# Attention rows fetched by indirect DMA and DMA transposes instead of one-hot matmuls, in blocks 1 to 7

## The chip, the cores and the metric

The kernel runs on one core of a Trainium2 chip. The metric is the device time of one execution in microseconds (us); the time of a kernel is the median of its runs. All times in the trace are microseconds from the start of the execution's span.

## The reference

The model is one layer over 16 sequences of 256 tokens with a vocabulary of 128 and a width of 512:

```python
h = rms_norm(rms_norm(emb[x]) * norm_w @ proj_w.T)          # depends on the token id only
h = h + attention(layernorm(h))                             # 16 heads of 32
h = h + ffn(layernorm(h))                                   # hidden 2048
# attention: q, k = feature_map(heads of h @ W.T);  scores = (q . k) ** 2, causal
# o = scores @ v / (sum(scores) + eps);  o @ Wo.T
# ffn: x = fwht(x * SU_ug) / 64;  silu(x @ Wg.T * s) * (x @ Wu.T * s);  fwht; x @ Wd.T
```

There are no positions in q and k, so the squared score of two tokens depends on their ids alone. A 128 x 128 table per head, id against id, holds every score that can occur. For a block of 512 tokens the attention of a head needs, for each query token, the row of the table that belongs to its id, weighted by how often each key id has occurred up to that token in its sequence.

## The kernel before

Tokens are worked on in 8 blocks of 512 (two sequences each). After a set-up stage that loads and turns the weights and builds the tables, an attention stage for block 0 runs alone (phase 0 below). Then in each step the feed-forward of block b runs beside the attention of block b + 1: step 0 also turns the rest of the weights (phase 1 below), steps 1 to 6 are a loop, and the last step has block 7's feed-forward alone. Each step is cut into 32 slots, and in every slot each engine's program holds the pieces of both tasks in a fixed, hand-written order; semaphores join the engines. Slots 0 to 15 hold the gate and up products of one 128-wide tile of the hidden layer (24 matmuls of 128x512 on TensorE, `feed_half`), slots 16 to 31 a quarter of an output tile of the down product (12 matmuls).

The attention table `att` holds each head's scores as two f16 halves, high and low, whose sum is the score. In the kernel before, TensorE picks the rows: `att[:, half, h, :]` against the one-hot matrix `onehotT` of the block's ids (L1215 and L1216, two matmuls of 128x512 a head, 16 heads a block). They add the halves in PSUM (`PICK`). Then for each head, one a slot:

- DVE multiplies the picked rows by the counts `cnt` into `prod` (L674), f32;
- ACT copies `prod` to the f16 high half in `p16` (L855), POOL subtracts for the low half (L358);
- at slots 4, 8, 12 and 15 TensorE multiplies a quad of four heads by the values (L1231, 48 small matmuls); DVE divides by the sums, ACT and POOL split the result into halves, and SP turns it with a DMA transpose (L276) for the output projection in slots 18 to 24.

Beside it the feed-forward of a slot runs TensorE (gate, up), ACT's silu (L993), DVE's product `a` (L743), ACT's high half and POOL's low half (L398). DVE's `a` of a slot waits for POOL's low half of the slot before, and TensorE's slot s + 2 waits for `a` of slot s.

In slots 17 to 29 the rest of attention (residual, layer norm, a Walsh-Hadamard turn) goes row tile by row tile: POOL gathers the residual rows by an indirect DMA (L387), DVE normalises, SP turns the tile by a DMA transpose (L283), TensorE mixes it. SP's queue is in order: four turns of the attention output, then turns of tiles between the stores of the output (L303).

Phase 1 is crowded on DVE: besides the product and `a` it splits turned weights (L477, L499) and mixes the down weights in place (L491, L492).

## Time and profile before

| | us |
|---|---|
| median of 3 runs | 1402.48 |
| lowest and highest | 1400.31, 1403.24 |
| the profiled execution's own time | 1400.2 |
| its span | 1398.4 |
| TensorE busy in the span | 1306.7 (93%) |
| VectorE (DVE), ScalarE (ACT), GpSimd (POOL) busy | 532.3, 398.7, 422.9 |
| one step of the loop (block 2 on), from the windows | 149.4 |

The busy share of TensorE is not spread evenly: the trace has set-up and phase 0 until about 163 us, phase 1 until about 372, six steps of about 149.5, and the last feed-forward. A matmul's own duration is longer than the distance at which matmuls follow one another, since they are pipelined; what a matmul costs a full TensorE is that distance. The mean granted TensorE clock is 0.974 of full speed.

### The profile page before, as it was taken

What the parts mean: (1) busy time and instruction counts of PE and PEld (TensorE: products, weight loads), DVE (VectorE), ACT (ScalarE), POOL (GpSimd) and SP (SyncE); (2) the same over time, 40 slices, a digit from 0 to 9 for tenths busy, and PEclk for the clock granted to TensorE, in tenths of its full rate; (3) what the DMA queues carried; (4) which work ended last, traced back from release to release, by engine and by line L of the source; (5) the groups of instructions that cost most, each with busy time, mean ns of one, the idle gap of its engine ahead of it and who ended that gap; (6) DMA issues with size and microseconds to landing.
All of it is one profiled execution on the core that took longest, in us unless ns stands there. A gap on an engine that the chain in (4) does not pass through costs nothing.

```text
span 1398.4 us, 19203 instructions
## 1 busy us (share of the span) xinstructions
PE 1306.7 (93%) x7481; PEld 643.6 (46%) x7481; DVE 532.3 (38%) x1049; ACT 398.7 (29%) x703; POOL 422.9 (30%) x371
## 2 busy tenths in 40 slices
PE   5575598989999999999999999999999999999999
PEld 3352255554444444444444444444444444444444
DVE  1655567654422253226222432234222523251110
ACT  4453463440233113321233023311322123211220
POOL 0342143332144313432244213421433124321210
PEclk9888699999999999999999999999999999999999
DMA  8911100002100130003000210012001300020000
GB/s 297 288 27 23 24 1 9 8 8 54 53 8 9 31 75 8 15 15 80 19 16 8 68 38 8 15 42 64 8 8 23 83 8 15 15 68 23 0 0 30
DMA packets 101681, 55.73 MB, mean 40 GB/s; under 512 B 74180, under 2 KB 90872, under 8 KB 101112
## 3 DMA queue, kind: packets, MB, share of 16 engines
q1 hardware_dynamic: 98112, 45.77, 12.8%
q0 software_dynamic: 2560, 8.39, 2.0%
q8 instruction: 43, 0.70, 0.2%
q10 hardware_dynamic: 952, 0.75, 0.2%
q14 instruction: 14, 0.11, 0.0%
HBM read 29.47 MB, written 8.65 MB: 27 GB/s over the span
## 4 chain that ended last, share of the span: by engine, by line
PE 83%; DVE 6%; DMA 4%; ACT 4%; issue 2%; POOL 1%; SPq 0%; DVEq 0%; ACTq 0%
PE bank L1078 24%; PE bank L1079 24%; PE bank L1080 23%; DMA prod<-sg 3%; PE bank L1231 3%; PE bank L1073 2%; PE bank L1216 2%; PE bank L1215 2%; PE bank L1121 1%; DMA hid<-in_L_tok_norm_weight 1%; PE bank L1240 1%; ACT xT L855 1%; DVE wgu L477 1%; PE bank L1071 1%; ACT wgu L855 1%
## 5 line engine op out<-in xcount | busy, mean ns | idle before, releaser
L1078 PE MATMUL bank<-xT,wgu 128*128 128x512 f16 x1024 | 389.3, 380 | 1.4 <-DVE xT L708 1.4
L1079 PE MATMUL bank<-xT,wgu 128*128 128x512 f16 x1024 | 389.3, 380 | 0.0
L1080 PE MATMUL bank<-xT,wgu 128*128 128x512 f16 x1024 | 389.2, 380 | 0.0
L398 POOL TENSOR_TENSOR hid<-a,hid 128x512 f16<-128x512 f32 x128 | 147.9, 1156 | 512.0 <-ACT hid L855 512.0
L743 DVE SCALAR_TENSOR_TENSOR a<-bank,kap,sg 128x512 f32<-128x512 f32 x128 | 96.0, 750 | 477.5 <-PE bank L1080 324.4
L1078 PE MATMUL bank<-wd,hid 128*128 128x512 f16 x512 | 194.3, 379 | 0.0
L1079 PE MATMUL bank<-wd,hid 128*128 128x512 f16 x512 | 194.1, 379 | 0.0
L1080 PE MATMUL bank<-wd,hid 128*128 128x512 f16 x512 | 194.0, 379 | 0.0
L358 POOL TENSOR_TENSOR p<-prod,p 128x512 f16<-128x512 f32 x128 | 153.2, 1199 | 128.4 <-ACT p L855 128.4
L855 ACT ACTIVATE hid<-a 128x512 f16<-128x512 f32 x128 | 80.6, 630 | 279.5 <-DVE a L743 279.5
L1080 PEld LDWEIGHTS bank<-xT,wgu 128*128 128x128 f16 x1024 | 100.4, 98 | 121.6 <-issue 1.4
L1078 PEld LDWEIGHTS bank<-xT,wgu 128*128 128x128 f16 x1024 | 100.6, 98 | 119.9 <-DVE xT L708 2.3
L1079 PEld LDWEIGHTS bank<-xT,wgu 128*128 128x128 f16 x1024 | 100.4, 98 | 116.9 <-issue 1.1
L993 ACT ACTIVATE sg<-bank,sc 128x512 f32<-128x512 f32 x128 | 87.2, 681 | 134.0 <-PE bank L1080 77.9
L855 ACT ACTIVATE p<-prod 128x512 f16<-128x512 f32 x128 | 79.6, 626 | 133.0 <-PE bank L1231 111.9
L855 ACT ACTIVATE sg<-wide,rstd 128x512 f16<-128x512 f32 x32 | 23.1, 722 | 273.8 <-DVE wide L449 226.5
L674 DVE TENSOR_TENSOR prod<-bank,cnt 128x512 f32<-128x512 f32 x128 | 86.6, 681 | 8.7 <-ACT cnt L855 8.0
L332 POOL TENSOR_TENSOR rstd<-ve,mhalf 128x1 f32<-128x1 f32 x32 | 32.3, 1009 | 155.9 <-DVE ve L726 155.9
L1080 PEld LDWEIGHTS bank<-wd,hid 128*128 128x128 f16 x512 | 50.2, 98 | 60.5 <-issue 0.3
L1079 PEld LDWEIGHTS bank<-wd,hid 128*128 128x128 f16 x512 | 50.1, 98 | 60.3 <-issue 0.7
L1078 PEld LDWEIGHTS bank<-wd,hid 128*128 128x128 f16 x512 | 50.1, 98 | 60.2 <-issue 0.7
L717 DVE SCALAR_TENSOR_TENSOR h<-bank,gl,h_row 128x512 f32 (+1 forms) x28 | 21.0, 749 | 106.6 <-DMA h_row<-h_table,ids_c 106.6
(178 smaller groups left out, 1245.8 us busy)
## 6 DMA issues: line engine op xcount, KB each, us to landing
out<-a SPq DMA_DIRECT2D x24, 256.0 KB, 2.2
wgu<-in_L_ffn_W_gate SPq DMA_DIRECT2D x16, 256.0 KB, 5.5
wgu<-in_L_ffn_W_up SPq DMA_DIRECT2D x16, 256.0 KB, 5.0
wd<-in_L_ffn_W_down SPq DMA_DIRECT2D x4, 1024.0 KB, 9.4
ids_b<-in_x SPq DMA_DIRECT2D x8, 256.0 KB, 3.5
out<-h_row SPq DMA_DIRECT2D x8, 256.0 KB, 2.0
xT<-in_L_tok_proj_weight SPq DMA_DIRECT2D x1, 1024.0 KB, 8.6
p<-in_L_attn_Wq SPq DMA_DIRECT2D x1, 1024.0 KB, 13.8
```

The source lines that it names most:

```text
L332: return nc.gpsimd.tensor_tensor(dst, src, mhalf[:, 0:src.shape[1]], ALU.pow)
L358: nc.gpsimd.tensor_tensor(p16[:, 1, h % 4, :], prod[:, h % 2, :], p16[:, 0, h % 4, :], ALU.subtract)\
L398: nc.gpsimd.tensor_tensor(hid[:, 1, s, :], a32[:, :], hid[:, 0, s, :], ALU.subtract)\
L674: nc.vector.tensor_tensor(prod[:, s % 2, :], PICK[s % 2][:, :], cnt[:, :], ALU.mult)\
L743: nc.vector.scalar_tensor_tensor(a32[:, :], bank[:, :], kap[:, s:s + 1], sg[:, :], ALU.mult, ALU.mult).then_inc(S["a_done"], 1)
L855: return nc.scalar.activation(dst, src, ACT.Copy, **kw)
L993: nc.scalar.activation(sg[:, :], bank[:, :], ACT.Silu, scale=sc[:, s:s + 1]).then_inc(S["silu_done"], 1)
L1073: last = mm(bank[:, i * P:(i + 1) * P], pieces(i), rights(i), start=True, stop=True)
L1078: mm(dst, w[0], v[0], start=first, stop=False)
L1079: mm(dst, w[0], v[1], start=False, stop=False)
L1080: return mm(dst, w[1], v[0], start=False, stop=final)
L1231: last = mm(HEADS[m // 2][:, 4 * (m % 2) + j, :], p16[:, p, j, m * P:(m + 1) * P], val[:, w, 4 * q + j, :], start=first, stop=final, skip_ ...
```

## The change

The four tables of a quad of heads (128 ids x 1024 f16 values: two halves of four heads) are stored once in DRAM (`att_tables`). For blocks 1 to 7, and each quad q and each tile m of 128 tokens, POOL gathers 128 rows of 2 KB by an indirect DMA into a staging buffer, and SP turns them by a DMA transpose into `PB[q % 2]`, which is the memory of `att` for even quads and `p16` for odd ones. That is 16 gathers and 16 turns a block. Quad 0 of the next block goes through the buffer `ids_b` at slots 12, 14, 18 and 25 (`NEXT_AT`); quads 1 to 3 use four pieces of `hid` that the feed-forward fills from slot 12 on, at slots 0 and 1, 3 and 4, 7 and 8 (`FETCH_AT`).

TensorE's picks of blocks 1 to 7 are left out (block 0 keeps them). DVE adds the two halves into `prod` and then multiplies by `cnt`: two operations in place of one, all operands in SBUF. DVE's one-hot of the ids by rows, and its load, stay for block 0 alone. POOL's loop over the steps 1 to 6 is written out, so that the numbers it waits for are constants.

```diff
@@ tables, stages @@
+        onehot = onehotT[:, :].rearrange("p (c v) -> p c v", c=4)
+        p_even = att[:, :, :, :].rearrange("p l h v -> p (l h v)").rearrange("p (l j t) -> p l j t", l=2, j=4)
+        PB = [p_even, p16]
+        stages = [ids_b[:, :].bitcast(F16)]
+        stages += [hid[:, l, f:f + 2, :].rearrange("p a b -> p (a b)") for f in (FT - 2, FT - 4) for l in range(2)]
+FETCH_AT = {0: ((1, 0), (1, 1)), 1: ((1, 2), (1, 3)), 3: ((2, 0), (2, 1)), 4: ((2, 2), (2, 3)),
+            7: ((3, 0), (3, 1)), 8: ((3, 2), (3, 3))}
+NEXT_AT = (12, 14, 18, 25)
@@ SP @@
+            def p_turn(n, q, m):
+                way, g = fetched(n, q, m)
+                sp.wait_ge(S[f"pg_land{way}"], 16 * g + 16)
+                if n == 1 and q == 0 and m == 0:
+                    sp.wait_ge(S["tab_stored"], 64)
+                    sp.wait_ge(S["picked"], H)
+                if m == 0 and (n, q) != (1, 0):
+                    sp.wait_ge(S["heads_ready"], QUADS * n + q - 1)
+                nc.sync.dma_start_transpose(PB[q % 2][:, :, :, m * P:(m + 1) * P].rearrange("p l j t -> p (l j) t"),
+                                            stages[way]).then_inc(S[f"pt_land{way}"], 16)
...
-            load_ids_rows(1)
+            load_gather_ids(1)
+            store_tables()
             for q in range(QUADS):
+                if q == 3:
+                    for m in range(2):
+                        p_turn(1, 0, m)
                 o_turn(0, q)
+            p_turn(1, 0, 2)
             for m in range(4):
+                if m == 3:
+                    p_turn(1, 0, 3)
                 x_turn(0, m)
@@ POOL @@
+            def gather(n, q, m):
+                way, g = fetched(n, q, m)
...
+                if q == 1 and m == 0 and not first(n - 1):
+                    pool.wait_ge(S["y_ready"], 4 * n - 4)
+                if not (first(n - 1) and (q == 1 or q == 0 and m == 0)):
+                    pool.wait_ge(S[f"pt_land{way}"], 16 * g)
+                nc.gpsimd.indirect_dma_start(stages[way], None, att_tables[q],
+                                             bass.IndirectOffsetOnAxis(ids_p[:, m:m + 1].bitcast(U32), axis=0))\
+                    .then_inc(S[f"pg_land{way}"], 16)
@@ DVE, product(n, s), blocks 1 to 7 @@
-                    nc.vector.tensor_tensor(prod[:, s % 2, :], PICK[s % 2][:, :], cnt[:, :], ALU.mult)\
+                        raw = PB[s // 4 % 2]
+                        if s % 4 == 0:
+                            for m in range(4) if s else (3,):
+                                way, g = fetched(n, s // 4, m)
+                                dve.wait_ge(S[f"pt_land{way}"], 16 * g + 16)
...
+                        nc.vector.tensor_tensor(prod[:, s % 2, :], raw[:, 0, s % 4, :], raw[:, 1, s % 4, :], ALU.add)\
+                            .then_inc(S["ps_done"], 1)
...
+                        nc.vector.tensor_tensor(prod[:, s % 2, :], prod[:, s % 2, :], cnt[:, :], ALU.mult)\
@@ TensorE, attend(n, s) @@
-                for h in (0, 1) if s == 0 else (s + 1,) if s + 1 < H else ():
+                for h in () if not zero else (0, 1) if s == 0 else (s + 1,) if s + 1 < H else ():
```

How the change moves instructions, at three places. TensorE in the loop, at the end of slot 0's up product, before:

```order
L1080 MATMUL bank<-xT,wgu 128x512
L1203 MATMUL bank<-c,p 128x256
L1204 MATMUL bank<-c,p 128x128
L1203 MATMUL bank<-c,p 128x256
L1204 MATMUL bank<-c,p 128x128
...
L1215 MATMUL bank<-onehotT,att 128x512
L1216 MATMUL bank<-onehotT,att 128x512
L1215 MATMUL bank<-onehotT,att 128x512
L1216 MATMUL bank<-onehotT,att 128x512
L1078 MATMUL bank<-xT,wgu 128x512
```

The same place after:

```order
L1305 MATMUL bank<-c,onehotT 128x256
L1306 MATMUL bank<-c,onehotT 128x128
L1305 MATMUL bank<-c,onehotT 128x256
L1306 MATMUL bank<-c,onehotT 128x128
L1178 MATMUL bank<-xT,wgu 128x512
```

The count matmuls stay, the four picks are gone; slots 1 to 14 of every block from 1 on lose two picks each in the same way.

DVE in phase 1, between the end of slot 5 and the start of slot 6 (`wd` is the down weights, `wgu` the gate and up weights, `a` the feed-forward's product), before:

```order
L491 TENSOR_TENSOR wd<-wd 128x2x512
L492 SCALAR_TENSOR_TENSOR wd<-wd 128x2x512
L674 TENSOR_TENSOR prod<-bank,cnt 128x512
L477 TENSOR_TENSOR wgu<-bank,wgu 128x512
L743 SCALAR_TENSOR_TENSOR a<-bank,kap,sg 128x512
```

and after:

```order
L567 TENSOR_TENSOR wd<-wd 128x2x512
L568 SCALAR_TENSOR_TENSOR wd<-wd 128x2x512
L765 TENSOR_TENSOR prod<-p 128x512
L770 TENSOR_TENSOR prod<-prod,cnt 128x512
L553 TENSOR_TENSOR wgu<-bank,wgu 128x512
L839 SCALAR_TENSOR_TENSOR a<-bank,kap,sg 128x512
```

The add L765 is a new row ahead of the multiplication, in front of the weight's low half and of `a`; the same happens in every slot from 0 to 15.

SP's queue for phase 0 (the turns of `h_row` and of `sg` are block 0's own attention output and tiles), before:

```order
L265 DMA ids_b<-in_x 128x512
L276 DMA_TRANSPOSE oT<-h_row 128x8x128 x4
L283 DMA_TRANSPOSE prod<-sg 128x8x128 x4
L270 DMA ids_c<-in_x 128x4x1
L276 DMA_TRANSPOSE oT<-h_row 128x8x128 x4
```

and after:

```order
L282 DMA att_table<-att 256x1x512 x4
L309 DMA_TRANSPOSE oT<-h_row 128x8x128 x3
L297 DMA_TRANSPOSE att<-ids_b 128x8x128 x2
L309 DMA_TRANSPOSE oT<-h_row 128x8x128
L297 DMA_TRANSPOSE att<-ids_b 128x8x128
L316 DMA_TRANSPOSE prod<-sg 128x8x128 x3
L297 DMA_TRANSPOSE att<-ids_b 128x8x128
L316 DMA_TRANSPOSE prod<-sg 128x8x128
L303 DMA ids_c<-in_x 128x4x1
L297 DMA_TRANSPOSE p<-hid 128x8x128 x4
```

Two of block 1's first four turns now stand ahead of the last turn of block 0's output, one ahead of the first tile's turn and one ahead of the last tile's.

## Rows read from the trace of the kernel before

**Rows 1.** The page: busy time by engine, and the chain that ended last.

```profile
PE 1306.7 (93%) x7481; PEld 643.6 (46%) x7481; DVE 532.3 (38%) x1049; ACT 398.7 (29%) x703; POOL 422.9 (30%) x371
...
PE 83%; DVE 6%; DMA 4%; ACT 4%; issue 2%; POOL 1%; SPq 0%; DVEq 0%; ACTq 0%
```

**Rows 2.** Windows, two loop steps: engines' busy us, clock, DMA share, GB/s.

```profile
522.50:671.90 149.40, 148.77 (x862) 69.93 (x860) 51.72 (x106) 37.73 (x61) 49.28 (x44) 1.00 0.13 30
671.90:821.30 149.40, 148.77 (x861) 69.81 (x860) 51.72 (x106) 37.73 (x61) 49.32 (x44) 1.00 0.12 31
```

**Rows 3.** Timeline of TensorE in a loop step: start, duration, instruction.

```profile
563.43 0.38 PE L1215 MATMUL bank<-onehotT,att 128*128 128x512 f16 x1
563.65 0.38 PE L1216 MATMUL bank<-onehotT,att 128*128 128x512 f16 x1
563.86 0.38 PE L1078 MATMUL bank<-xT,wgu 128*128 128x512 f16 x1
```

**Rows 4.** The gathers L387: min/median/max ns, and landing.

```profile
L387 POOL DMA_INDIRECT h_row<-h_table,ids_c x28: 998/1054/1063, 329.1 to 1247.9; - x28
...
DMA to landing us min/median/max: 3.2/3.4/3.5
```

**Rows 5.** The DMA transposes L283: SP's ns, and landing.

```profile
L283 SPq DMA_TRANSPOSE prod<-sg x32: 1232/1238/1298, 137.2 to 1261.9; - x32
...
DMA to landing us min/median/max: 3.0/3.1/3.8
```

**Rows 6.** Timelines of POOL and DVE in a loop step's first slots.

```profile
642.54 1.05 POOL L387 DMA_INDIRECT h_row<-h_table,ids_c  x1 [0.18 <-issue]
...
679.03 1.16 POOL L398 TENSOR_TENSOR hid<-a,hid 128x512 f16<-128x512 f32 x1 [22.40 <-ACT hid L855]
681.14 2.27 POOL L358 TENSOR_TENSOR p<-prod,p 128x512 f16<-128x512 f32 x2 [0.95 <-ACT p L855]
...
691.00 1.15 POOL L398 TENSOR_TENSOR hid<-a,hid 128x512 f16<-128x512 f32 x1 [3.34 <-ACT hid L855]
692.11 1.15 POOL L358 TENSOR_TENSOR p<-prod,p 128x512 f16<-128x512 f32 x1
...
689.50 0.75 DVE L743 SCALAR_TENSOR_TENSOR a<-bank,kap,sg 128x512 f32<-128x512 f32 x1 [4.26 <-PE bank L1080]
690.17 0.68 DVE L674 TENSOR_TENSOR prod<-bank,cnt 128x512 f32<-128x512 f32 x1
695.12 0.75 DVE L743 SCALAR_TENSOR_TENSOR a<-bank,kap,sg 128x512 f32<-128x512 f32 x1 [4.26 <-PE bank L1080]
```

**Rows 7.** Chain of waits in phase 0: start, duration, what.

```profile
117.54 1.16 POOL p L358
...
123.57 3.04 DMA oT<-h_row
...
157.16 3.10 DMA prod<-sg
```

**Rows 8.** Timelines of SP and POOL in phase 0.

```profile
113.18 11.62 SPq L276 DMA_TRANSPOSE oT<-h_row  x2
...
154.12 1.65 POOL L336 TENSOR_TENSOR h<-h,mhalf 128x8 f32<-128x8 f32 x1 [1.34 <-DVE h L456]
```

**Rows 9.** Windows of phase 1, slots 1 to 7: columns as in rows 2.

```profile
188.00:240.00 52.00, 47.80 (x306) 27.87 (x305) 41.62 (x76) 23.44 (x47) 21.02 (x16) 1.00 0.03 6
```

**Rows 10.** Timeline of DVE in phase 1, slots 5, 6 and 10.

```profile
216.54 0.68 DVE L471 TENSOR_TENSOR h<-h 128x512 f32<-128x512 f32 x1
...
220.95 0.68 DVE L674 TENSOR_TENSOR prod<-bank,cnt 128x512 f32<-128x512 f32 x1
...
259.25 0.75 DVE L743 SCALAR_TENSOR_TENSOR a<-bank,kap,sg 128x512 f32<-128x512 f32 x1 [1.85 <-issue]
```

**Rows 11.** Timelines of DVE and POOL in phase 1, where both read SBUF twice.

```profile
252.84 1.22 DVE L491 TENSOR_TENSOR wd<-wd 128x1024 f32<-128x1024 f32 x1
254.09 2.06 DVE L492 SCALAR_TENSOR_TENSOR wd<-wd 128x1024 f32<-128x1024 f32 x1
...
253.22 1.84 POOL L358 TENSOR_TENSOR p<-prod,p 128x512 f16<-128x512 f32 x1 [0.42 <-ACT p L855]
```

**Rows 12.** Waits of TensorE in phase 1: us in total, times, longest.

```profile
PE bank L1121 <- DVE wd L499: 2.1, 1, 2.1
```

More of the change, by code:

```diff
@@ L96, in tower @@
         h_table = nc.dram_tensor("h_table", [VOCAB, D], F32, kind="Internal").ap()
+        att_tables = [nc.dram_tensor(f"att_table{q}", [VOCAB, 8 * P], F16, kind="Internal").ap() for q in range(QUADS)]
         wgu = sb("wgu", [P, GROUPS, DC, 2, 512], F16)
@@ L289, in block_io @@
                     if turning is not None:
+                        for m in range(4):
+                            if q < 3:
+                                p_turn(turning, q + 1, m)
+                            elif turning < NB - 1 and m < 2:
+                                p_turn(turning + 1, 0, m)
+                        if q == 2 and turning < NB - 1:
+                            load_gather_ids(turning + 1)
                         o_turn(turning, q)
+                if turning is not None and turning < NB - 1:
+                    p_turn(turning + 1, 0, 2)
                 if turning is not None:
@@ L293, in block_io @@
                 for m in range(4):
-                    if n is not None and m == 2:
-                        load_ids_rows(n)
+                    if m == 3 and turning is not None and turning < NB - 1:
+                        p_turn(turning + 1, 0, 3)
                     if n is not None and m == 3:
@@ L357, in product, with fetch @@
                     pool.wait_ge(S["ph_done"], H * n + h + 1)
-                    nc.gpsimd.tensor_tensor(p16[:, 1, h % 4, :], prod[:, h % 2, :], p16[:, 0, h % 4, :], ALU.subtract)\
+                    p = p16 if first(n) else PB[h // 4 % 2]
+                    nc.gpsimd.tensor_tensor(p[:, 1, h % 4, :], prod[:, h % 2, :], p[:, 0, h % 4, :], ALU.subtract)\
                         .then_inc(S["pl_done"], 1)
+            def gather(n, q, m):
+                way, g = fetched(n, q, m)
+                pool.wait_ge(S["h_stored"], 16)
+                pool.wait_ge(S["idp_land"], 16 * n)
+                if first(n - 1) and q == 0:
+                    if m == 0:
+                        pool.wait_ge(S["tab_stored"], 64)
+                        pool.wait_ge(S["onehotT_ready"], 1)
+                if q == 1 and m == 0 and not first(n - 1):
[5 more added lines that the diff above has]
+                    .then_inc(S[f"pg_land{way}"], 16)
+            def fetch(n, s):
+                for q, m in FETCH_AT.get(s, ()):
+                    gather(n, q, m)
+                if s in NEXT_AT and not (isinstance(n, int) and n == NB - 1):
+                    gather(n + 1, 0, NEXT_AT.index(s))
             def first(n):
@@ L402, in _ @@
                 product(0, s)
+                if s in NEXT_AT:
+                    gather(1, 0, NEXT_AT.index(s))
                 attend(0, s)
@@ L426, in _ @@
                     bound_power(2)
-            with pool.Fori(1, NB - 1) as b:
+            for b in range(1, NB - 1):
                 for s in range(SLOTS):
+                    fetch(b + 1, s)
                     pair(b, s)
@@ L551, in ids @@
             def ids(n):
[L552 to L555 removed]
+                zero = isinstance(n, int) and n == 0
+                if zero:
+                    dve.wait_ge(S["ids_land"], 16)
+                    nc.vector.tensor_scalar(onehotT[:, :], ids_b[:, :], iota_col, None, ALU.is_equal)\
+                        .then_inc(S["onehotT_ready"], 1)
+                else:
+                    dve.wait_ge(S["picked"], H)
+                    dve.wait_ge(S["count_ready"], n)
                 dve.wait_ge(S["idc_land"], 16 * (n + 1))
@@ L946, in product @@
                     act.wait_ge(S["p_done"], i + 1)
-                    if s % 4 == 0:
-                        act.wait_ge(S["heads_ready"], QUADS * n + s // 4)
-                    copy(p16[:, 0, s % 4, :], prod[:, s % 2, :]).then_inc(S["ph_done"], 1)
+                    zero = isinstance(n, int) and n == 0
+                    if zero and s % 4 == 0:
+                        act.wait_ge(S["heads_ready"], s // 4)
+                    copy((p16 if zero else PB[s // 4 % 2])[:, 0, s % 4, :], prod[:, s % 2, :]).then_inc(S["ph_done"], 1)
             def attend(n, s):
@@ L996, in feed_high @@
                 if s < FT:
+                    if s == FT - 4 and not (isinstance(b, int) and b == NB - 1):
+                        for way in range(1, 5):
+                            act.wait_ge(S[f"pt_land{way}"], 48 * (b + 1))
                     act.wait_ge(S["a_done"], FT * b + s + 1)
@@ L1195, in attend @@
             def attend(n, s):
+                zero = isinstance(n, int) and n == 0
+                tokens = onehot0 if zero else onehot
                 if s == 0:
@@ L1230, in attend @@
                                 final = m % 2 == 1 and j == 3 and p == 1
-                                last = mm(HEADS[m // 2][:, 4 * (m % 2) + j, :], p16[:, p, j, m * P:(m + 1) * P],
+                                last = mm(HEADS[m // 2][:, 4 * (m % 2) + j, :], (p16 if zero else PB[q % 2])[:, p, j, m * P:(m + 1) * P],
                                           val[:, w, 4 * q + j, :], start=first, stop=final, skip_group_check=True)
```

59 lines of the change are left out of this document (36 added, 23 removed).

## The prediction

> **What bounds the kernel now.** I read the page first: TensorE is busy 93% of the span and makes up 83% of the chain that ended last [rows 1]. An average over stages says little, so I cut the span by windows. In a step of the loop (149.4 us) TensorE is busy 148.77 us at a clock of 1.00, while DVE has 51.7, ACT 37.7 and POOL 49.3 [rows 2]. Six of the eight attention blocks that could change (2 to 7) lie in such steps. The reader is to see that there nothing but TensorE's own instructions counts: what it no longer executes comes off the step, as long as no other engine grows to 142 us or makes TensorE wait. Two stretches are of another kind. Phase 0 is a chain through DVE, ACT, POOL and DMAs, in which the turns on SP's queue stand themselves [rows 7]. Phase 1 is balanced: in its slots 1 to 7 TensorE has 47.8 us of 52.0 and DVE 41.6 [rows 9], and with the dependent steps between DVE's operations there is little air on either.
>
> **The picks.** In the loop a pick begins 0.22 us after the one before, and the next product's matmul 0.21 after the last: 563.43, 563.65, 563.86, so 0.215 each [rows 3]; the 0.38 beside them is the length of a pipelined matmul and not its price. A block has 32 of them: 32 x 0.2155 = 6.9 us a step, and six steps give 41.4. For block 1, in phase 1, it is 6.9 at most. Block 0 keeps its picks. The count matmuls, the small matmuls of the quads and the output projection stay.
>
> **What replaces them in a loop step.** A slot of feed-forward lasts 24 x 0.2155 = 5.2 us after the change (5.6 now, 695.12 - 689.50 [rows 6]).
>
> - DVE: 16 adds more. The nearest row with two SBUF inputs of that size took 0.68 us (L471 [rows 10]), and the product reading PSUM also 0.68 [rows 6]. So 16 x 0.68 = 10.9 us: DVE goes from 51.7 to about 63 of 142. A slot then has 0.75 + 0.68 + 0.68 = 2.1 of 5.2. Hidden by the 4.26 us for which DVE waits for TensorE before each `a` [rows 6].
> - POOL: 16 gathers more. The same instruction with the same 128 rows of 2 KB took 1.05 us on POOL [rows 4], with 0.18 ahead of it [rows 6]: 1.24 each, 19.8 a step, POOL goes to 69 of 142. The densest slots have two: 2.5 + 2.3 (its two subtractions, 691.00 to 693.3) = 4.8 of 5.2, and 5.9 where a quad's output adds a third subtraction. And a delay has to be long to be seen: POOL's L398 ends 2.5 us before the `a` that needs it (692.15 against 695.12, less the 0.43 of picks), and TensorE asks for that `a` only 5.2 - 0.75 = 4.4 later. Slack 6.9 us. Cost 0.
> - The way of quad 1, the shortest. Zero is the step's start at 671.9. POOL's first two gathers go at once, the last two behind its first two subtractions: POOL's first L358 ends at 682.3 [rows 6], less 0.9 of picks, so they run from 681.6 to 684.1 and the last lands 3.4 us after its start [rows 4], at 686.3. Its turn lands 3.1 later [rows 5], at 689.4, which is 17.5 from zero. DVE comes to the first head of quad 1 behind the `a` of slot 3, at 695.9 less the 1.7 us of the four pairs of picks before it, 22.3 from zero. The margin is 4.8 us, and a late product would first have to use up 4.5 more before TensorE misses `a` of slot 4. Quads 2 and 3 have wider margins, since their gathers start four slots ahead of use and wait only for a quad's matmuls to free the buffer. Cost 0.
> - SP: 16 turns more at 1.24 us [rows 5], 19.8 us of issuing in 142. In slots 17 to 29 only two of them stand among the tiles' turns: one waits for a gather that POOL issues right behind the first tile's residual gather and that lands 1.24 us after it, while DVE still has that tile's whole normalisation to do before its turn can be asked for; the other stands behind the last tile's turn. Cost 0.
>
> **Collisions of DVE and POOL.** Where DVE worked in place on two SBUF operands while POOL subtracted, both were stretched: L492 took 2.06 us against 1.22 for its neighbour L491, and POOL's L358 in the same moment 1.84 against its usual 1.15 [rows 11, 6]. Now the add and the multiplication both have two SBUF inputs, where the old product had one in PSUM. In a loop slot they can meet POOL's L398, which begins 1.5 us after `a` starts; one of the two then waits up to 1.15 us. Inside the 4.26 us that costs nothing. The Trainium skill has this as a rule ("SBUF — State Buffer", section on who interferes with whom): a DVE instruction with two SBUF inputs and a GpSimd instruction that reads SBUF exclude each other for a whole instruction. The trace agrees by the two stretched rows, and by the rule alone every slot would lose up to one subtraction on DVE, still not TensorE's bound.
>
> **Phase 1.** TensorE saves 6.9 us at most. DVE has a row more in each slot, in front of the weight's low half, for which TensorE's next turn waits, and of `a` [the order above]. In slots 1 to 7 DVE has 41.6 of 52 us busy and waits otherwise mostly for ACT's half of the weight just turned [rows 9]; a slot grows by between 0 and 0.68 + 0.43. I take +0.4 each, 2.8. In slot 13, where DVE holds TensorE up by 2.1 us already [rows 12], +0.7. In the other eight slots DVE still has some 1.85 us ahead of `a` (259.25 [rows 10]) and the picks are saved: 0.43 a slot, with two pairs in slot 0, 9 pairs, less 3.9; but product 15 passes a chain that is longer by the add, +0.7, and collisions of rows 11's kind cost something, +0.7. Sum +1.0. Bounds: -6.9, if DVE's air holds all, and +16 x (0.68 + 0.5) less 3.9, about +15, if every slot takes the add and half a collision.
>
> **Phase 0.** Here SP's new turns stand on the chain.
>
> - The second gather of block 1 needs the first one's turn landed. That turn goes behind SP's third output turn: 113.18 + 1.24 = 114.4 [rows 8, 5], lands at 117.5, and the gather ends at 118.6. POOL's subtraction for the last head was at 117.54, on the chain [rows 7]: +1.1. The turn that stands ahead of the output's last one is issued at 118.6 - 1.05 + 3.4 = 121.0 and is done on SP at 122.3, before 123.57 + 1.1: no more.
> - The fourth gather stands behind POOL's power at 154.12 + 1.65 = 155.8, with the shift 156.9; from 157.1 it lands at 160.5. Its turn takes SP 1.3 us, and the last tile's turn goes at 161.8 instead of 157.16 + 1.1 = 158.3 [rows 7, 8]: +3.5. That turn is on the chain, so both count: 4.6 us. Bounds: 0, if the landing of the tables and gathers falls earlier than I think, and 8, if the second turn waits for the first one's 3.1 in full.
> - The store of the four tables, 1 MB, stands before anything on SP needs its time. 0.
>
> **The sum.** Against the profiled execution's own time: 1400.2 - 41.4 + 4.6 + 1.0 = 1364.4. The median of the runs is 2.3 above that execution, so 1366.7; I give 1366.5.
>
> **The rivals.**
>
> - Everything hides: phase 0 takes its turns free and phase 1 saves all its picks. 1400.2 - 48.3 + 2.3 = 1354. For it speaks DVE's share of 0.8 in phase 1; against it that two new turns are issued by a gather which itself comes late. Chance 0.10.
> - Collisions decide in phase 1 and at the last quad: slots 1 to 7 and 13 take one subtraction of 1.15 us each besides, 8 x 1.15 = 9.2, and in the six loop steps the last quad, whose product has only its own slot, loses some 0.5 each, 3. 1366.5 + 12 = 1379. The rule of the Trainium skill named above would bring this about; the rows show it for the long mixes, and most of POOL's subtractions in phase 1 fall beside these, not beside the product. Chance 0.14.
> - The fetches of one quad do not overlap: gather, turn, gather, turn, at 3.4 + 3.1 each. Quad 1 is then there 4 x 6.5 + 1 = 27 us after the step's start, where `a` of slot 4 is due at 26.7 (695.12 + 5.6 less 671.9 and 2.1 of picks) and TensorE needs it by 4.4 later; with DVE's product in between it loses up to 1 us a step, and the chain in phase 0 some 4 more. 1366.5 + 6 + 4 = 1376. Against it: four buffers, each with its own count. Chance 0.07.
> - Slower: the gathers hold POOL much longer than 1.05 us when 16 of them a block read other tables. With c for one gather, a pair of dense slots runs behind by 2 x (2c + 2.3 - 5.2), less the slack of 6.9, three times a step. It eats the 6.9 us of picks from c = 3.75 us on; at c = 4 it is 3 x 3.3 = 9.9 a step, 59 in all, and the time 1425. Against it stand 28 gathers between 998 and 1063 ns, some of them beside DVE work. Chance 0.06.
> - The change does nothing, because TensorE's steps are held by something that the trace files under TensorE: a step's 149.4 us would stay. But a step has 148.77 us of matmuls back to back; chance 0.02, time 1402.
>
> The forecast itself has 0.61. Its own range is 1360 to 1373. With the rivals on both sides the range for 8 in 10 is 1356 to 1382. A difference of less than 0.2%, 2.8 us, could not be told from none here. Faster by more than that: 0.61 + 0.10 + 0.14 + 0.07 = 0.92; within: 0.02; slower: 0.06.
>
> **What would show it.** Loop steps of 142.5 us with TensorE busy all but 0.7; DVE near 63 and POOL near 69 a step; no wait of DVE for a turn of `att` or `p16`; the last tile's turn of phase 0 on the chain, started near 162; phase 1 from its first matmul to its end within 2 us of now. I am wrong if a loop step keeps more than 143.5, if DVE's first product of a quad waits for a DMA, or if phase 1 grows by more than 4 us.

## The result, and the profile after

| | before | after |
|---|---|---|
| median, us | 1402.62 (1400.31 to 1403.24, 4 runs) | 1382.5 (1379.77 to 1382.88, 4 runs) |
| ratio, 95% interval | | 0.9855, 0.9838 to 0.9872 |
| the profiled execution, its span | 1400.2, 1398.4 | 1382.7, 1380.9 |

The change saves 1.45%, or 17.5 us between the profiled executions, where I had forecast 35.8. By stage, each measured from the first matmul of one feed-forward to the first of the next:

| | before | forecast | after |
|---|---|---|---|
| start to the end of phase 0 | 162.75 | +4.6 | 171.94 (+9.2) |
| phase 1 | 209.75 | +1.0 | 212.47 (+2.7) |
| first loop step | 150.12 | -6.9 | 143.52 (-6.6) |
| loop steps 2 to 6, mean | 149.60 | -6.9 | 145.04 (-4.6) |
| last feed-forward | 127.79 | 0 | 127.78 |

The page after, the same lines as in [rows 1]: TensorE lost 224 matmuls and 44 us, DVE gained 129 us, POOL 142, and "issue" rose from 2% of the chain to 5%. Of these 3%, some 40 us, the pauses told below are 8.

```profile
PE 1262.6 (91%) x7257; PEld 619.9 (45%) x7257; DVE 660.9 (48%) x1154; ACT 398.2 (29%) x703; POOL 565.2 (41%) x483
...
PE 76%; DVE 9%; issue 5%; DMA 4%; ACT 4%; POOL 2%; SPq 0%; DVEq 0%; POOLq 0%; ACTq 0%
```

Two loop steps in the columns of [rows 2]. POOL has the 70 us that I had counted; DVE has 71 and not 63. TensorE's busy time fell by 6.35 us, and yet the step is 145.5 us and not 142.5: 3 us of it TensorE is idle, where it was 0.6.

```profile
527.90:673.50 145.60, 142.42 (x828) 66.59 (x828) 71.36 (x122) 37.63 (x61) 70.32 (x60) 1.00 0.41 87
673.50:818.90 145.40, 142.43 (x829) 66.64 (x830) 71.00 (x121) 37.63 (x61) 70.02 (x60) 1.00 0.41 88
```

What TensorE waited for in the six loop steps (us in total, times, longest). In the kernel before there is no row with "issue" in this stretch and none with POOL.

```profile
PE bank L1178 <- issue: 8.2, 6, 1.9
PE bank L1339 <- DMA prod<-sg: 4.0, 6, 0.7
PE bank L1330 <- POOL p L408: 1.9, 5, 0.5
```

The first row is a pause that begins 1.5 us, six matmuls, behind each of the loop's five jumps back to its start, 8.0 us in the five (the sixth piece is 0.2 us ahead of one step's first matmul). No semaphore belongs to it. TensorE's timeline at two of them:

```profile
527.93 0.39 PE L1178 MATMUL bank<-xT,wgu 128*128 128x512 f16 x1
...
531.01 0.39 PE L1178 MATMUL bank<-xT,wgu 128*128 128x512 f16 x1 [1.62 <-issue]
...
676.89 0.39 PE L1178 MATMUL bank<-xT,wgu 128*128 128x512 f16 x1 [1.90 <-issue]
```

The third row is a wait of the last quad's small matmuls for POOL. It is the end of a short chain, which one step shows. SP issues the third turn of the attention output and, behind it, the turn of the next block's first tile; then POOL's second gather, which reuses that tile's buffer, sits idle for the turn; POOL's next two operations are late, and its L470 now falls on DVE's add and multiplication of slot 15, which take 1.34 and 1.53 us for 0.68 and 0.69. Timelines of SP, POOL, DVE and TensorE:

```profile
604.53 1.24 SPq L309 DMA_TRANSPOSE oT<-h_row  x1
605.87 1.38 SPq L297 DMA_TRANSPOSE att<-ids_b  x1
...
610.92 0.97 POOL L423 DMA_INDIRECT ids_b<-att_table,ids_p  x1 [1.38 <-DMA att<-ids_b]
611.91 1.16 POOL L408 TENSOR_TENSOR p<-prod,p 128x512 f16<-128x512 f32 x1
613.12 1.53 POOL L470 TENSOR_TENSOR hid<-a,hid 128x512 f16<-128x512 f32 x1
...
612.29 1.34 DVE L765 TENSOR_TENSOR prod<-p 128x512 f32<-128x512 f16 x1
613.67 1.53 DVE L770 TENSOR_TENSOR prod<-prod,cnt 128x512 f32<-128x512 f32 x1
...
617.23 1.38 PE L1330 MATMUL bank<-val,p 128*128 128x33 f16 x48 [0.51 <-POOL p L408]
```

Phase 0, the chain of waits, in the columns of [rows 7] and beside them. Each of the steps that I had named is there, and each cost more than I had put.

```profile
119.47 0.97 POOL ids_b L423
120.46 1.17 POOL p L408
...
126.51 4.29 DMA oT<-h_row
...
160.47 3.85 DMA ids_b<-att_table,ids_p
164.33 1.23 SPq L297
165.65 3.79 DMA prod<-sg
...
171.94 0.61 PE bank L1178
```

### The profile page after: what moved, and what is told of

Read it like the earlier page. It is cut to its first block, busy times and chain, and to the rows that moved or that the text cites. A ratio compares the mean times of both kernels' runs of the same rounds, so it can differ in the third digit from the quotient of the medians.

```text
span 1380.9 us, 18955 instructions
## 1 busy us (share of the span) xinstructions
PE 1262.6 (91%) x7257; PEld 619.9 (45%) x7257; DVE 660.9 (48%) x1154; ACT 398.2 (29%) x703; POOL 565.2 (41%) x483
## 4 chain that ended last, share of the span: by engine, by line
PE 76%; DVE 9%; issue 5%; DMA 4%; ACT 4%; POOL 2%; SPq 0%; DVEq 0%; POOLq 0%; ACTq 0%
PE bank L1178 23%; PE bank L1180 23%; PE bank L1179 23%; PE bank L1330 3%; DMA prod<-sg 2%; PE bank L1173 2%; DVE wd L568 1%; POOL p L408 1%; PE bank L1221 1%; DMA hid<-in_L_tok_norm_weight 1%; DVE wd L567 1%; DVE wgu L553 1%; DVE prod L765 1%; ACT p L951 1%; PE bank L1171 1%
## 5 line engine op out<-in xcount | busy, mean ns | idle before, releaser
L470 POOL TENSOR_TENSOR hid<-a,hid 128x512 f16<-128x512 f32 x128 | 172.7, 1349 | 289.0 <-ACT hid L951 288.4
L839 DVE SCALAR_TENSOR_TENSOR a<-bank,kap,sg 128x512 f32<-128x512 f32 x128 | 96.1, 751 | 320.4 <-PE bank L1180 305.4
L423 POOL DMA_INDIRECT hid<-att_table,ids_p x84 | 85.3, 1016 | 111.0 <-PE bank L1180 91.8
L770 DVE TENSOR_TENSOR prod<-prod,cnt 128x512 f32<-128x512 f32 x112 | 111.2, 993 | 7.8 <-ACT cnt L951 4.0
L951 ACT ACTIVATE sg<-wide,rstd 128x512 f16<-128x512 f32 x32 | 23.2, 724 | 274.0 <-DVE wide L525 178.7
L408 POOL TENSOR_TENSOR p<-prod,p 128x512 f16<-128x512 f32 x72 | 84.5, 1174 | 42.7 <-ACT p L951 42.2
L408 POOL TENSOR_TENSOR att<-prod,att 128x512 f16<-128x512 f32 x56 | 71.3, 1274 | 20.3 <-ACT att L951 20.1
```

Of the source, the lines that this page charges most:

```text
L408: nc.gpsimd.tensor_tensor(p[:, 1, h % 4, :], prod[:, h % 2, :], p[:, 0, h % 4, :], ALU.subtract)\
L423: nc.gpsimd.indirect_dma_start(stages[way], None, att_tables[q], bass.IndirectOffsetOnAxis(ids_p[:, m:m + 1].bitcast(U32), axis=0))\
L470: nc.gpsimd.tensor_tensor(hid[:, 1, s, :], a32[:, :], hid[:, 0, s, :], ALU.subtract)\
L770: nc.vector.tensor_tensor(prod[:, s % 2, :], prod[:, s % 2, :], cnt[:, :], ALU.mult)\
L839: nc.vector.scalar_tensor_tensor(a32[:, :], bank[:, :], kap[:, s:s + 1], sg[:, :], ALU.mult, ALU.mult).then_inc(S["a_done"], 1)
L951: return nc.scalar.activation(dst, src, ACT.Copy, **kw)
```

## The experiments

Each time is a median of two runs where no other number is given, and each ratio is to runs of the kernel before on the same chip. Stages are measured as in the table above.

**All four gathers of quad 1 in one slot.** The first idea on the pause was that the fetches at the step's start had to do with it.

```diff
-FETCH_AT = {0: ((1, 0), (1, 1)), 1: ((1, 2), (1, 3)), 3: ((2, 0), (2, 1)), 4: ((2, 2), (2, 3)),
+FETCH_AT = {1: ((1, 0), (1, 1), (1, 2), (1, 3)), 3: ((2, 0), (2, 1)), 4: ((2, 2), (2, 3)),
```

> All four gathers of quad 1 go in slot 1, none in slot 0. In the changed kernel's trace TensorE stands 1.2 to 1.9 us six matmuls after each of the loop's five backward jumps, with no wait on any engine. Theory A (the fetch of TensorE's instructions after the jump queues behind the gathers' 512 KB on the same DMA engines): the pause goes at all five jumps, loop steps 2 to 6 shrink from 145.0 to about 143.4 us each, the time falls by 8 to 10 us to about 1373. Rival B (the pause comes from something else of the change, POOL's written-out loop or the later buffers): the pause stays at 1.2 to 1.9 and the time stays within 1381 to 1383. In both, POOL is 2.5 us later in slot 1 and quad 1 lands later; if that were dear, the steps would grow.

1378.4 us, ratio 0.9834 (0.9801 to 0.9868). The pauses stay at 1.62, 1.28, 1.49, 1.52 and 1.52 us although slot 0 holds no gather any more; loop steps 2 to 6 have 144.9 on average. So POOL's gathers of the step's start are not the cause. The time is 4 us lower all the same, and 3.0 of that is phase 0, which the edit does not touch: it ended at 168.9 here and at 171.9 in the changed kernel. In the kernels below that leave phase 0 and TensorE's start alone it ends between 170.1 and 171.7. So a difference of 3 us in a total can come from there alone, and the stages have to be compared.

**Phase 0 in another order.** The four turns of block 1 go behind the last output turn and between the tiles' turns, and their gathers to slots 12, 19, 23 and 25.

```diff
+FIRST_AT = (12, 19, 23, 25)
@@ SP, phase 0 @@
-                if q == 3:
-                    for m in range(2):
-                        p_turn(1, 0, m)
                 o_turn(0, q)
+            p_turn(1, 0, 0)
+            x_turn(0, 0)
+            p_turn(1, 0, 1)
+            x_turn(0, 1)
+            x_turn(0, 2)
             p_turn(1, 0, 2)
-            for m in range(4):
-                if m == 3:
-                    p_turn(1, 0, 3)
-                x_turn(0, m)
+            x_turn(0, 3)
+            p_turn(1, 0, 3)
```

> Only block 0's stage is changed: on SP the four turns for block 1 go behind block 0's last output turn, behind the first and the third tile's turn and behind the last tile's turn; POOL's gathers go in slots 12, 19, 23 and 25. Theory A (the turns and gathers stood on the chain of phase 0): TensorE's first feed-forward matmul comes at 163 to 165 us instead of 171.9, time about 1375. Rival B (most of the 9.2 us come from earlier, or from transfers that get in each other's way wherever they stand): it comes at 168 or later and the time is above 1379.

1373.1 us, ratio 0.9797 (0.9764 to 0.983). The feed-forward begins at 163.2, where it was 162.75 before the change. The chain has the lone output turn again, and the last tile's turn 9 us earlier:

```profile
122.95 3.25 DMA oT<-h_row
...
156.65 4.06 DMA prod<-sg
...
163.20 0.61 PE bank L1179
```

So nearly all of what phase 0 had grown, 6.2 to 9.2 us in the executions with the first order, was the place of these four turns and their gathers. Phase 1 (212.3) and the pauses are unmoved.

**The add one product earlier on DVE.**

```diff
+            def add_ahead(n, s):
+                if 2 <= s < H and s % 4:
+                    add_halves(n, s)
...
+                    add_ahead(b + 1, s + 1)
```

> In the loop the add of a head (but for the first of a quad and the first two) stands one product earlier on DVE, ahead of the a of the slot before; nothing else. Theory A (the last quad's matmuls wait 0.5 us because head 15's add and product both collide with POOL's subtraction and stand in one row): the wait at the last quad goes, its matmuls fall from 1.38 to 1.2 us, each loop step is 0.5 to 0.9 us shorter, time about 1378. Rival B (the wait has another cause, such as POOL's gather in slot 14): the wait stays, time 1381 to 1383.

1378.7 us, ratio 0.9836 (0.9802 to 0.9871). The last quad waits in two steps of six instead of five, for 0.62 and 0.40 us; the loop is 1.5 us shorter in all and phase 1 keeps its 212.5. It moves little: 1.9 of the 3.9 us are phase 0, which ended at 170.1.

**TensorE's loop written out.** The same instructions, no jump.

```diff
-            with pe.Fori(1, NB - 1) as b:
+            for b in range(1, NB - 1):
```

> TensorE's loop over the steps 1 to 6 is written out, so that it has no backward jump; the gathers stay in slot 0. Theory A (the pause is a fetch after a jump): no pause of over 0.5 us at any step's start, time 1371 to 1375, unless straight fetches also fall behind the transfers, which would show as pauses elsewhere. Rival B (the pause comes from what the gathers do to TensorE's data, or from a wait): it stays at 1.2 to 1.9 us a step and the time at 1381 to 1383.

1370.1 us, ratio 0.9775 (0.972 to 0.983). The two runs are 5.2 us apart, so the time says less than the stages. No pause is left, and four of six steps have 142.5 to 142.7 us: the pause belongs to the jump. But two steps have 144.3 and 144.0, each with a wait of the last quad for POOL, of 1.34 and 1.11 us. So these waits have another cause than the jump itself.

**Without the add.** The low halves are left out: DVE multiplies the high half alone.

```diff
-                        nc.vector.tensor_tensor(prod[:, s % 2, :], raw[:, 0, s % 4, :], raw[:, 1, s % 4, :], ALU.add)\
-                            .then_inc(S["ps_done"], 1)
-                        nc.vector.tensor_tensor(prod[:, s % 2, :], prod[:, s % 2, :], cnt[:, :], ALU.mult)\
+                        nc.vector.tensor_tensor(prod[:, s % 2, :], raw[:, 0, s % 4, :], cnt[:, :], ALU.mult)\
```

> The low halves of the scores are left out in blocks 1 to 7: DVE multiplies the high half by the counts and adds nothing, so one of the two new rows a head is gone; everything else stays. Theory (the add costs phase 1 its growth and makes the wait at the last quad): phase 1 falls from 212.5 us to 206 to 208, the last quad's wait of 0.2 to 0.5 us goes, the pauses of 1.2 to 1.9 us after the jumps stay; time 1374 to 1377. Rival (phase 1's growth comes from the transfers or from product and subtraction colliding alone): phase 1 stays above 210.

1373.3 us, ratio 0.9776 (0.9747 to 0.9804). Phase 1 takes 208.6, so the add costs 3.9 us there, where I had put 3.5 for slots 1 to 7 and 13, and 1.4 for the last product and the collisions. The 3.9 is more than what phase 1 had grown by (2.7); the theory on record asked for more still (206 to 208). In the loop the last quad's wait is gone, the pauses stay at 1.27 to 1.46, and loop steps 2 to 6 still have 144.2.

**Only blocks 2 to 7 fetched.** Block 1 keeps its picks; the rest follows from one number, with gathers and turns of block 1 taken out of phase 0 and phase 1, and the one-hot of its ids by rows put back.

```diff
+FIRST = 2
...
-                for q, m in FETCH_AT.get(s, ()):
+                for q, m in FETCH_AT.get(s, ()) if n >= FIRST else ():
```

> Block 1 keeps TensorE's picks as block 0 does, and the gathers and turns begin with block 2. Phase 0 should be back at 163 us and phase 1 at 209.8 (both as before), so 1382.5 - 9.2 - 2.7 = 1370.6 if the pauses after the jumps stay (theory: gathers, turns or the shorter loop cause them), and 1361 if they go (theory: the place of the loop's first instruction in TensorE's program decides, which here is the same as in the kernel before, since phase 1 has its 64 pick instructions again).

1358.9 us, ratio 0.9673 (0.9645 to 0.9702). Phase 0 ends at 162.8 and phase 1 takes 210.8. Of the two cases on record, the second came: loop steps 2 to 6 have 142.5 to 142.8 us, with no pause and no wait for POOL, although their instructions are those of the changed kernel. What differs for TensorE is what stands ahead of the loop: 67 instructions more, the picks of block 1 and their waits. But block 1's fetches are gone too, so this kernel alone does not tell the two apart. The next two kernels move nothing but the loop's place.

**67 instructions more ahead of the loop.** The wait for a constant that landed long ago is written 134 times more at the head of TensorE's program, which makes 67 instructions.

```diff
-            pe.wait_ge(S["c_land"], 16)
+            for _ in range(134 + 1):
+                pe.wait_ge(S["c_land"], 16)
```

> The changed kernel with 67 instructions more at the very start of TensorE's program (waits on a semaphore that is long there), where TensorE idles. They put the loop's first instruction where it stands in the kernel before. Theory (the place decides: in the changed kernel a block of instructions ends some 16 instructions after the jump's target and the next one is not there yet): no pause after the jumps, loop steps 2 to 6 of 143 to 143.5 us, time 1372 to 1374. Rival (the transfers beside it, or the shorter loop body): the pause stays at 1.2 to 1.9 us and the time at 1380 to 1383.

1369.7 us, ratio 0.9751 (0.9722 to 0.9779): with idle instructions added the kernel is 13 us faster, 11.6 of it in the loop. Loop steps 2 to 6 have 142.4 to 142.8. Phase 1 is 0.9 us longer than without them and the first loop step 0.3; phase 0 ended 2.0 earlier, within its scatter. The waits of TensorE in the loop, and the slot that was shown above, where the same SP and POOL instructions find their turn landed and L470 misses the multiplication:

```profile
PE bank L1340 <- DMA prod<-sg: 3.8, 6, 0.7
PE bank L1340 <- DVE xT L804: 1.3, 1, 1.3
```

```profile
603.22 1.28 SPq L297 DMA_TRANSPOSE att<-ids_b  x1
...
607.08 0.97 POOL L423 DMA_INDIRECT ids_b<-att_table,ids_p  x1 [0.18 <-issue]
...
609.65 0.68 DVE L765 TENSOR_TENSOR prod<-p 128x512 f32<-128x512 f16 x1
610.36 0.69 DVE L770 TENSOR_TENSOR prod<-prod,cnt 128x512 f32<-128x512 f32 x1
```

**The kernel before with 189 instructions more.** The same waits, 378 of them, in the kernel before: no fetch by DMA in it, but its loop now starts where the changed kernel's does, by a count in blocks of 256 instructions.

```diff
-            pe.wait_ge(S["c_land"], 16)
+            for _ in range(378 + 1):
+                pe.wait_ge(S["c_land"], 16)
```

> The kernel before with 189 such instructions at the start of TensorE's program, which puts the loop's first instruction where it stands in the changed kernel if what counts repeats every 256 instructions. Theory (the place decides): a pause of 1.2 to 1.9 us after each of the five jumps in a kernel without any of the new gathers or turns, time 1408 to 1412. Rival (it takes the new transfers or the shorter body): no pause, time 1400 to 1403.

1421.9 us, ratio 1.0122 (1.0093 to 1.0152). The recorded 1408 to 1412 had no term for the padding itself. Between the two profiled executions the time grows by 23.2 us: phase 0 ends 12.6 later, and the loop steps grow too, to 151.6 on average for steps 2 to 6 (149.6 before), and the pauses are there:

```profile
PE bank L1078 <- issue: 8.3, 5, 1.9
```

So the pause needs none of the new fetches. The changed kernel got it by having less code ahead of its loop.

**What the DMA rows say of it.** The queue of instructions is a row in the view of DMA. Its columns are packets, MB and share of 16 engines. The kernel before, in the loop steps that begin at 672.1 and 821.5:

```profile
q8 instruction: 7, 0.11, 0.3%
...
q8 instruction: 2, 0.03, 0.1%
```

The changed kernel, in the step that begins at 673.5; the kernel before with the 189 has the same line in its own:

```profile
q8 instruction: 9, 0.15, 0.4%
```

The changed kernel with 67 more has no such row at all in the step from 669.7 to 812.4, and the one with TensorE's loop written out has 6 or 7. Over the whole span the packets of 16 KB are 43 before, 70 after, 25 with the 67, 71 with the 189. A step of TensorE is about 1700 recorded instructions: 828 weight loads, as many matmuls and some 40 of its sequencer. Where the loop lies well, its code stays in the engine from step to step; where it lies badly, all of it is read again in every step, and the piece that is needed six matmuls behind the jump is not there yet. That the pause is this wait can be read from the times, by windows of 0.2 us. In the changed kernel one packet begins 2.5 to 2.9 us ahead of each jump and the next 0.3 to 1.0 us behind it, and takes 0.9 to 1.4. TensorE goes on 1.3 to 1.5 us after its end, so that the pause is 1.2 us where that packet ended early and 1.9 where it ended late; in seven kernels with the pause it is 1.2 to 1.6 us, all 35 times. Ahead of the pause of 1.90 us, from 674.4 to 674.6:

```profile
q8 instruction: 1, 0.02, 27.4%
```

The kernel before stood between the two: 7 packets and 2 in turn, one reading of the code in two steps, and no pause.

The same fetches go with the last quad's waits. The stretch from 604.4 to 611.0 of the changed kernel, with the two turns of the chain above in it:

```profile
q1 hardware_dynamic: 2112, 0.52, 65.2%
q8 instruction: 1, 0.02, 0.9%
...
oT<-h_row SPq DMA_TRANSPOSE x1, 4.9
```

and the same 6.6 us of a step of the kernel with the 67:

```profile
q1 hardware_dynamic: 2112, 0.52, 42.4%
...
oT<-h_row SPq DMA_TRANSPOSE x1, 3.3
```

One packet of code among the 2112 packets of the two turns, and the output's turn lands after 4.9 us instead of 3.3. It is so in all five steps in which the changed kernel has two such turns, each with a packet of code in them: 4.5 to 4.9 us. In the kernels with 67 and 32 instructions more, without a packet, the same turns took 3.2 to 3.3. In the loop POOL's second gather into `ids_b` waits for its turn in five steps of the changed kernel (1.1 to 1.4 us), in two where TensorE's loop is written out (2.03 and 1.78), and in none of the kernel with the 67 and of the one from block 2. Step by step these are the ones in which TensorE then waits for POOL: 0.40, 0.51, 0.22, 0.28 and 0.46 us in the one, 1.34 and 1.11 in the other. That the packet stretches the turn is read from the traces; the padding took all packets of a step away at once, and no run was made to move that packet alone. But chance moved it once in the kernel with 256 instructions more (below): in one of its five steps the packet came 80.7 us into the step, behind the turn, and not at some 79. There the turn took 3.3 us, and TensorE did not wait for POOL; in the other four it took 4.6 to 4.9, and TensorE waited.

**One more block, and half a dose.** Two kernels with a single run each, on where the loop has to lie.

```diff
-            pe.wait_ge(S["c_land"], 16)
+            for _ in range(512 + 1):
+                pe.wait_ge(S["c_land"], 16)
```

> The changed kernel with 256 instructions more at the head of TensorE's program (67 more took the pauses away). Theory A (what counts is the place of the jump's target within a block of 256 instructions): the pauses of 1.2 to 1.9 us after each of the five jumps are back, loop steps 2 to 6 of 144.5 to 145.6; the start some 12 us later, so 1395 in all. Rival B (any padding takes them away, by the length of the program or the shift of its start): no pause, loop steps of 142.7, and 1382.

1398.0 us: phase 0 ends 16.3 us later than in the changed kernel, where I had put 12. The pauses are back, 7.5 us in five, the longest 1.9, and so are four waits for POOL, 9 packets of code in the step from 833.6 to 978.6, and loop steps 2 to 6 of 144.2 to 145.5.

```profile
PE bank L1178 <- issue: 7.5, 5, 1.9
PE bank L1340 <- DMA prod<-sg: 4.6, 7, 0.7
PE bank L1331 <- POOL p L408: 1.6, 4, 0.5
```

> The changed kernel with 32 instructions more at the head of TensorE's program, half of what took the pauses away. The pause stood some 7 feed-forward matmuls behind the jump. Theory A (the pause comes where the instructions that stand ready from the target on run out, and its length falls with every instruction that they reach further or less far): the pause is there, but shorter or at another matmul: 0.3 to 1.5 us. Rival B (only two cases, by the block that the target lies in): the pause stays at 1.2 to 1.9 us and at the same matmul, or it is gone altogether.

(The edit is that of the 256, with 64 waits.) 1371.6 us: no pause, no packet of code in a step, loop steps 2 to 6 of 142.5 to 142.7. Half the dose does all, and theory A, a shorter pause, is out. The table has what stands ahead of the loop in TensorE's program as it is written, each matmul counted as two. (The traces record every matmul of the set-up on f32 data twice and so have about 3506 for the 2990; the remainders are then 178, 210 and 245, and the rows part in the same way.)

| kernel | instructions ahead | less whole 256s | pauses |
|---|---|---|---|
| after; in other slots, without the add | 2990 | 174 | yes |
| after + 256 | 3246 | 174 | yes |
| before + 189 | 3246 | 174 | yes |
| after + 32 | 3022 | 206 | no |
| after + 67; from block 2; before | 3057 | 241 | no |

Padding as such (rival B of the 256) is out, since 32 and 67 help and 256 does not. The loop's place decides, and a shift by 256 gives the same place again. Only three places were tried, so the period could be a part of 256, and where the bad stretch begins and ends is not known. Of degrees there is no sign: the pause begins behind the same six matmuls in every kernel that has it.

**Both cures on the kernel of the change.** Phase 0's order as above and the 67 instructions.

> The changed kernel, block 1 fetched too, with two edits that each gave something alone: block 1's first four turns and gathers at other places of phase 0 (alone 1373.1), and 67 instructions more at the head of TensorE's program (alone 1369.7). Theory A (two separate causes, so the gains add): 1373.1 - 5 x 1.5 (pauses) - 6 x 0.4 (waits for POOL at the last quad) + up to 4 for the padding at the start = 1363 to 1367, phase 0 ending at 163 to 167, loop steps of 142.7. Rival B (the earlier start of the loop only brings the fetches closer to the time they are needed, and they are late again): loop steps over 143.5, 1370.

1363.3 us (1362.3 to 1364.7, 5 runs), ratio 0.9717 (0.9701 to 0.9732). Phase 0 ends at 164.3, loop steps 2 to 6 take 142.5 to 142.8, and phase 1 takes 213.4, which with the 67 is again 0.9 more than without. The gains add, as theory A had them.

**From block 2, with the earlier add.**

> Block 1 keeps its picks, blocks 2 to 7 fetch their rows, and the add of the two halves stands one product earlier on DVE. Theory A (what the fetch costs lies in phase 0, in phase 1 and in the place of the loop's first instruction; with the old code ahead of the loop all three are as in the kernel before): 1358 us, within 2 us of the same kernel without the earlier add (1358.9), loop steps of 142.5 to 142.8, phase 0 ending at 163, no pause on TensorE after the loop's jumps. Rival B (the add placed earlier makes a quad's first head late, since it stands in front of the feed-forward's product): loop steps of 143.2 or more, 1362.

1359.6 us (1357.9 to 1360.3, 5 runs), ratio 0.9691 (0.9675 to 0.9706), loop steps of 142.7 again. There the gather waits 0.8 us for its turn in five steps, without a packet of code, and TensorE does not. The time can't be told from the kernel from block 2 without the earlier add (1358.9). These two are the fastest, 3.1 to 3.3% below the kernel before and 1.7% below the changed one.

## Why the prediction was wrong

The sign was right and the time was not: 16 us above my 1366.5 and just outside the range. Between the two spans the miss is 12.0 us in the loop, 4.6 in phase 0 and 1.7 in phase 1.

- **"Six steps give 41.4": the price was right, the sum incomplete.** 6.9 us a step is what the picks cost: the kernels without the pause have loop steps of 142.4 to 142.8 where I forecast 142.5. In the changed kernel they save 29.4 us. The step that failed is the sentence that in a loop step "nothing but TensorE's own instructions counts", so that a step gives back all that it no longer executes. Removing block 1's picks moved the loop's place among the blocks of code, and the sum has no term for that. Of the 12.0 us missing in the loop, the pauses are 8.0 and the last quad's waits 1.9; the rest is that TensorE itself is busy for 142.4 us of a step, where with the 67 instructions it is 141.9. The 67 give back 11.6 in the loop.
- **"With 148.77 us of matmuls back to back"** was read as a property of the loop. It was one of the loop where it lay. The view of DMA of the kernel before had the warning, 7 packets of code in one step and 2 in the next: the loop's code just about stayed in the engine. I had not read that row. The Trainium skill ("Runtime: NRT & Kernel Launch", section on instruction fetch mechanics) says that code comes in blocks of 256 instructions, mostly hidden, and that a taken branch to a block outside the current window of two stalls until it is fetched. The runs agree with the first: 6 or 7 packets a step and no pause without the jump. With the second they agree in part: with 9 packets a step there is a stall of 1.2 to 1.9 us at each jump, but it comes six matmuls behind the target and not at it, and whether it comes depends on the target's place.
- **"Cost 0" for gathers, turns and adds in a loop step**: true in the padded kernels, with DVE at 70 and POOL at 70 us of 142.7 (in the one with the 67). It was not quite true beside fetches of code. The margins that I worked out for quads 1 to 3 held, as no product waited for a turn; the weak place was the second gather of quad 0, whose buffer has one tile and for which I counted no margin, and behind it the product of slot 15, which my second rival had named at "some 0.5 each". It waited 0.4.
- **DVE at 63** was 71: 8 us a step more. The add and the multiplication have means of 0.87 and 1.03 us and not 0.68, as they meet POOL's subtractions. That is the exclusion that I had cited, at its place: [rows 11]'s kind of stretch, up to 1.34 and 1.53 us in the slot shown. TensorE saw only the last one.
- **Phase 0, +4.6.** The mechanism was right, and every term of it was too small. Of the 9.2, 1.0 was there before the first of the new turns (106.56 for 105.53 in the chain, 117.16 for 116.12 at the last head's product) and so is the execution's. The last head's subtraction came 1.9 later than that and not 1.1: the first turn took the 3.1 us of [rows 5] from its issue, but POOL's gather began 0.74 us behind the end of its wait for it, for which I had no term. The last output turn took 4.29 instead of 3.04 [rows 7], another 1.25: block 1's second turn had landed by then (POOL's wait for it ended at 125.87, the output turn went at 126.51), and what ran beside it was the third gather, issued 0.12 us later, which took 4.33 itself. The rest is the fourth gather and its turn, 4.3 instead of 3.5, and the last tile's turn, 3.79 instead of 3.10. That is the 9.2. Durations of transfers that ran alone were mostly put on transfers that run beside another. The bound of 8 was too low by these terms and the execution's 1.0.
- **Phase 1, +1.0** came out at +2.7, inside the bounds. The add is 3.9 of it. TensorE's wait for the weights' low half (L477 before, L553 now) grew from 1.4 us in 3 to 7.4 in 6, and the one of [rows 12] from 2.1 to 2.4, so slot 13 paid less than 0.7. By the starts of `a` (L743 before, L839 now), slots 1 to 7 grew by 5.3 us instead of 2.8 and slot 8, for which I had a saving, by 1.7; from slot 9 on most slots came out 0.4 shorter, as forecast. Block 1's whole 6.9 us of picks come to nothing: with them kept, phases 0 and 1 together are 11 us shorter.

The rival "collisions decide", 1379, came nearest in time and was not the cause: it wanted 9.2 us more from slots 1 to 7 and 13 of phase 1, where they gave less than 2 more than forecast. The fetches of a quad did overlap. What I said would show me wrong, a loop step over 143.5, did.

What stays open is why 174 is bad and 206 and 241 are good. An estimate, with blocks of 256 as named above: if a block ends at the pause, some 13 instructions behind the loop's first, the loop of 1700 lies in 8 blocks, and started 32 or 67 later in 7. That would go with all or nothing of it being read again, and paddings just short of 13 and just beyond it would test it; no run did. The kernel before comes to 8 by the same count and has 7 and 2 packets in turn, so the estimate is not the whole of it. Open is also how far a fetch of code beside a turn stretches it by itself, and why padding costs 0.9 us in phase 1.

## What to carry to other kernels

When an edit adds or removes instructions ahead of a hardware loop on the engine that sets the time, read the instruction queue's packets in one loop step, before and after: if the loop's code is fetched anew in every step, some idle instructions ahead of the loop may give back a good part of what the edit was worth (here 13 us beside 20), and a comparison of two edits without that look compares where their loops lie. A transfer that is put beside one on the critical chain costs more than its issue: it makes the other longer too, so take the duration of pairs and not of lone ones. And a replacement that pays in the steady loop need not be made in the crowded stage ahead of it: leaving block 1 as it was gives 1358.9 us by itself, where both repairs with block 1 fetched give 1363.3.

## What the runs showed of the hardware

- The jump back of TensorE's loop of about 1700 instructions costs nothing or 1.2 to 1.9 us, by where the loop begins: 32 or 67 instructions more ahead took it away, 256 brought it back, and 189 more gave it to a kernel that had none.
- Where the loop lies well, no packet of code is fetched in a step of 142.7 us; where it lies badly, 9 of 16 KB. TensorE's pause ends 1.2 to 1.6 us after the end of the packet fetched behind the jump.
- The turn of 256 KB took 3.2 to 3.3 us from issue to landing, and 4.5 to 4.9 with one packet of code in it. With a gather of 256 KB issued 0.12 us behind it, it took 4.29.
- Waits at the head of TensorE's program are not free: 378 of them moved its first matmul from 13.2 to 24.8 us; 134 of them did not delay it, as TensorE had to wait for its first operand anyway. Two such waits make one instruction, and one followed the other after 0.106 us.
